# Blocks of zero matmuls on TensorE at four places of a one-core attention and feed-forward kernel

## Chip, cores and metric

The kernel runs on one core of a Trainium2 chip. The metric is the device time of one execution in microseconds (us), as the median of the runs. Engines are called PE (TensorE), DVE (VectorE), ACT (ScalarE), POOL (GpSimd) and SP (SyncE, here the engine that issues most DMAs); PEld is PE's weight load. PE's clock has two levels, 1.2 and 2.4 GHz; the profile shows the granted one as a fraction of full speed.

## What is computed

One layer on x of shape (2, 2048, 256): differential attention with 16 heads of width 16 (two score maps per head, values of width 32), then a gated feed-forward net with ternary weights, each followed by a residual sum and a layer norm. Cut to what matters:

```python
q1, q2, k1, k2 = (heads(x @ W) for W in (Wq1, Wq2, Wk1, Wk2)); v = heads(x @ Wv)
a1 = softmax(causal(q1 @ k1.T * scale)); a2 = softmax(causal(q2 @ k2.T * scale))
out = (a1 - lam * a2) @ v
out = (out - mean(out)) / sqrt(var(out) + eps) * (1 - LAM_INIT)
x = layernorm(x + merge(out) @ Wo)
h = silu((x @ w1.T) * s1) * ((x @ w2.T) * s2)
h = gelu((h @ h1.T) * hs1); h = gelu((h @ h2.T) * hs2)
x = layernorm(x + (h @ w3.T) * s3)
```

## The kernel before

The program is a row of phases, each a block with one instruction list per engine, written out by hand; between two blocks all engines meet at a barrier. The order on an engine is the order of the code, and engines wait for each other by semaphores only.

**Projection** (`project_phase`). The 4096 tokens are cut into 8 tiles of 512. For each tile PE makes eight m-tiles (q1, q2, k1, k2, two halves of 128 columns each), every one of six matmuls 128 x 512: two chunks of the width 256 by three passes, as each f32 operand is cut into a high and a low part (L479). It writes them to four PSUM banks in turn, so the fifth m-tile must wait until ACT has copied the first one out (L349). Between them come the four value tiles of L490. ACT makes the high parts of x (L333), wqk (L338) and wv (L340), DVE the low parts (L374, L378, L415); ahead of ACT's cast of wv DVE centres wv (L410, L412). ACT's queue has the cast of wv ahead of the first copy. At the end DVE takes the largest projection, POOL reduces it over the partitions (L324), and DVE sets a flag, `exact`, and the shift.

**The test of the exact path** (`maximum_phase`). Each engine loads the flag; when it is set, an extra phase finds the true row maxima. With these inputs it is not run, and only the load and the branch remain.

**Attention** (`attention_phase`). For each of 16 heads, PE makes scores into three PSUM slots (`scores`, L934), ACT takes the exponential of each (L908), POOL masks the corners on the diagonal (L880), and PE weighs the values (`weigh`, L957), DVE copies the sums, PE turns them (`turn`, L965), DVE finishes them. For the first head, the scores wait until DVE has added the shift to q (L1037). In the last head parts of the next stage for the first 512 tokens are done early: transposes (L977, L999) and the output projection (L987). The last thing on PE is the turn of the last query tile.

**Finish** (`finish_phase`). Each engine loads a second flag, `wide`. Then for 8 tiles of 512 tokens: the up-projections (L1525, 64 matmuls 128 x 512), two hidden layers (L1541, 256 matmuls), the down-projection (L1558), with the output projection and norm of the next tile in between. Small buffers of the norms come from `norm_buffers`.

Of the kernel before, what the change touches and what calls it, by code (L numbers as in the profile page):

```python
# [66 lines left out]
def layer_kernel(nc, x, xt, wqk, wv, wo, lq1, lk1, lq2, lk2, ffn, scales, s3, out):  # L67
# [7 lines left out]
    with ExitStack() as ctx:  # L75
        def sb(name, shape, dt=F32):
            return ctx.enter_context(nc.sbuf_tensor(name, shape, dt))

        keep = dict(
            scales=sb("scales", [PARTS, 4, HC]), counts=sb("counts", [PARTS, 2 * CHUNKS]), wide_col=sb("wide_col", [PARTS, 2]),
            s3=sb("s3", [PARTS, EMBED]),
            ident=sb("ident", [PARTS, PARTS]), neg_lam=sb("neg_lam", [PARTS, HEADS]),
            bound=sb("bound", [PARTS, 2]), exact=sb("exact", [PARTS, 1], I32), wide=sb("wide", [PARTS, 1], I32),
            low_rows=sb("low_rows", [PARTS, 2]), shift_row=sb("shift_row", [PARTS, 1]), safe_row=sb("safe_row", [PARTS, 1]),
            shift_add=sb("shift_add", [PARTS, 1]), query_rows=sb("query_rows", [PARTS, 1]),
        )
        for n, name in enumerate(("s1", "s2", "hs1", "hs2")):
            keep[name] = keep["scales"][:, n, :]  # L90
        finish = ctx.enter_context(Room(nc, "finish"))
        sems, finish_credits = finish_sems(finish)
        max_sems, max_credits = maximum_sems(finish)
        attn_sems, attn_credits = attention_sems(finish)
        with ExitStack() as weights:

            whole = weights.enter_context(nc.sbuf_tensor("ffn_r", [PARTS, CHUNKS, CHUNK], F32R))
            rounded = ffn_views(whole)
            early = early_buffers(nc)
            with Room(nc, "heads") as room:  # L100
                heads = first_head_buffers(room)
                project_phase(nc, keep, whole, heads, xt, wqk, wv, (lq1, lk1, lq2, lk2), ffn, (scales, s3),
                              qk_raw, values, shift, ones, finish_credits + max_credits + attn_credits)
                more_head_buffers(room, heads)
                maximum_phase(nc, keep, max_sems, heads, qk_raw, shift, ones)
                attention_phase(nc, keep, attn_sems, heads, early, qk_raw, shift, ones, values, ffn, whole, x, wo, diffs)
            finish_phase(nc, keep, sems, "split", True, rounded, early, attn_sems["stored"], x, wo, diffs, out)
        whole_w = sb("ffn_f", [PARTS, CHUNKS, CHUNK])
        load_weights_phase(nc, keep, ffn, whole_w)
        finish_phase(nc, keep, sems, "full", False, ffn_views(whole_w), None, attn_sems["stored"], x, wo, diffs, out)  # L110
# [30 lines left out]
        return self.ctx.enter_context(self.nc.Block())  # L141


def give_credits(eng, credits):

    for sem, n in credits:
        eng.sem_inc(sem, n)  # L147


def project_phase(nc, keep, rounded, heads, xt_in, wqk_in, wv_in, lam_in, ffn, ffn_s, qk_raw, values, shift, ones, later_credits):  # L150
# [13 lines left out]
    with Room(nc, "proj") as room:  # L164
# [25 lines left out]
        scales_loaded = room.sem("scales_loaded")  # L190
        x_loaded = [room.sem(f"x_loaded{u}") for u in range(2)]
        w_loaded = [room.sem(f"w_loaded{n}") for n in range(STAGES)]
        ident_done = room.sem("ident_done")
        preset_set = room.sem("preset_set")
        ones_stored = room.sem("ones_stored")
# [175 lines left out]
        def _(dve):  # L371
# [22 lines left out]
            def mark_rows():  # L394
# [6 lines left out]
                dve.wait_ge(row_vec, 2)  # L401
                nc.vector.scalar_tensor_tensor(keep["low_rows"][:, :], row_sums[:, :, 0], -1.0, row_sums[:, :, 1], ALU.mult, ALU.subtract).then_inc(row_vec, 1)

            low_x(0)
            for n in range(len(KINDS)):
                low_w(n)
# [55 lines left out]

        @block.tensor
        def _(pe):
            for t in range(TILES):

                pe.wait_ge(xt_ready, t + 1)
                for m in range(M_TILES):
# [14 lines left out]
                    if s is not None:  # L483
                        if t == 0:
                            pe.wait_ge(wv_ready, 1)
                        else:
                            pe.wait_ge(v_copied, SUBS * (t - 1) + s + 1)
                        for c in range(EC):
                            for i, (a, b) in enumerate(PASSES):
                                last = nc.tensor.matmul(v_ps[s][:, :, :], xt[t % 2][b][:, c, s * PARTS:(s + 1) * PARTS], wv[a][:, c * HEADS:(c + 1) * HEADS, :],  # L490
                                                        start=(c == 0 and i == 0), stop=(c == EC - 1 and i == len(PASSES) - 1))
                        last.then_inc(v_projected, 1)


def cut_piece(nc, dve, raw, stack, high, low_rows, made_high, i, made):
# [196 lines left out]

PROBS = 4
EARLY_PASSES = [(0, 0), (1, 0), (0, 1)]
EARLY_COLUMNS = 8448


def early_buffers(nc):
# [14 lines left out]

def norm_buffers(room, which):

    return dict(
        stats=room.sb(f"{which}_stats", [PARTS, SUBS, 6]), mean_var=room.sb(f"{which}_mean_var", [PARTS, SUBS, 2]),
        var=room.sb(f"{which}_var", [PARTS, SUBS]), root=room.sb(f"{which}_root", [PARTS, SUBS]),
        quotient=room.sb(f"{which}_quotient", [PARTS, SUBS]), rstd=room.sb(f"{which}_rstd", [PARTS, SUBS]),
    )  # L720


def attention_sems(room):
# [13 lines left out]
def attention_phase(nc, keep, sems, heads, early, qk_raw, shift, ones, values, ffn, rounded, x, wo, diffs):  # L737
# [44 lines left out]
    with Room(nc, "attn") as room:  # L782
# [128 lines left out]
        def _(pe):  # L911
# [105 lines left out]
            def head(h, u, r, first, last):  # L1017
# [5 lines left out]
                if last:  # L1023
                    for k in range(NS - LAG, NS):
                        use(h, u, first, k)
                    turn(h, QUERY_TILES - 1)

            all_heads(head)

        @block.vector  # L1030
# [817 lines left out]
```

## Time and profile before

| | us |
|---|---|
| median of 3 runs | 1936.9 |
| lowest, highest | 1936.12, 1937.7 |
| the profiled execution, its time | 1934.14 |
| the profiled execution, its span | 1932.4 |
| PE busy | 1858.1 |
| ACT busy | 1408.5 |
| DVE busy | 1027.1 |
| mean granted clock of PE | 0.985 |

The profile page, the chain of waits and the timeline come from that one execution. In a timeline row the first number is the start, the second the duration, both in us from the start of the span; then come the engine, the line, the operation, what it writes and reads, its shape and its count, and in brackets how long the engine was idle before it and what ended that. Rows of several instructions (x8) are merged: the duration is that of the whole. A name with q (SPq) is the engine's queue, here issuing DMAs. A row of windows gives a stretch, its length, the busy time of PE, PEld, DVE, ACT and POOL with the number of instructions, the granted clock of PE, the share of the DMA engines and GB/s. A clock of 0.50 is 1.2 GHz and 1.00 is 2.4 GHz; a number in between says at which point of the stretch it changed.

### The profile page before, as it was taken

What the parts mean: (1) busy time and instruction counts of PE and PEld (TensorE: products, weight loads), DVE (VectorE), ACT (ScalarE), POOL (GpSimd) and SP (SyncE); (2) the same over time, 40 slices, a digit from 0 to 9 for tenths busy, and PEclk for the clock granted to TensorE, in tenths of its full rate; (3) what the DMA queues carried; (4) which work ended last, traced back from release to release, by engine and by line L of the source; (5) the groups of instructions that cost most, each with busy time, mean ns of one, the idle gap of its engine ahead of it and who ended that gap; (6) DMA issues with size and microseconds to landing.
All of it is one profiled execution on the core that took longest, in us unless ns stands there. A gap on an engine that the chain in (4) does not pass through costs nothing. (4 is left out here: it accounts for less than half of the span.)

```text
span 1932.4 us, 30772 instructions
## 1 busy us (share of the span) xinstructions
PE 1858.1 (96%) x12160; PEld 1063.5 (55%) x12160; DVE 1027.1 (53%) x1985; ACT 1408.5 (73%) x1701; POOL 247.8 (13%) x311
## 2 busy tenths in 40 slices
PE   7997999999999999999999967999999999999996
PEld 6773333333333333333333323888888888888885
DVE  5555655555655665565555543535445454536342
ACT  4546999999999999999999965535445454535452
POOL 3001111211121111111122130000000000000000
PEclk9998999999999999999999988999999999999998
DMA  8877156534663357435653420010010001010000
GB/s 275 251 251 153 24 103 115 93 70 85 115 118 62 73 111 121 81 70 97 115 99 69 81 54 12 33 33 14 31 33 12 33 12 33 12 33 22 1 11 13
DMA packets 130143, 146.08 MB, mean 76 GB/s; under 512 B 74228, under 2 KB 100468, under 8 KB 122356
## 3 DMA queue, kind: packets, MB, share of 16 engines
q1 hardware_dynamic: 129272, 142.46, 34.1%
q8 instruction: 99, 1.62, 0.4%
q10 hardware_dynamic: 720, 1.57, 0.2%
q14 instruction: 52, 0.43, 0.1%
HBM read 101.79 MB, written 39.06 MB: 73 GB/s over the span
## 5 line engine op out<-in xcount | busy, mean ns | idle before, releaser
L908 ACT ACTIVATE attn_probs<-attn_s_ps 128x1024 f32<-128x1024 f32 x1088 | 1002.8, 1128 | 36.3 <-PE attn_s_ps L934 35.9
L957 PE MATMUL attn_sums_ps<-attn_probs,heads_v 128*32 128x512 f32 (+3 forms) x5120 | 589.8, 542 | 14.2 <-POOL attn_probs L880 14.2
L934 PE MATMUL attn_s_ps<-heads_q,heads_k 50*128 50x512 f32 (+3 forms) x2560 | 451.2, 427 | 12.5 <-DVE heads_q L1037 12.1
L934 PEld LDWEIGHTS attn_s_ps<-heads_q,heads_k 50*128 50x128 f32 x2560 | 213.1, 185 | 448.4 <-ACT attn_probs L908 401.7
L1627 ACT ACTIVATE split_whole<-split_hid_ps,scales 128x512 f32<-128x512 f32 x128 | 88.3, 690 | 274.2 <-PE split_hid_ps L1541 274.1
L880 POOL TENSOR_SCALAR_AFFINE_SELECT attn_probs<-attn_probs 128x512 f32<-128x512 f32 x256 | 182.9, 726 | 816.5 <-ACT attn_probs L908 816.5
L1541 PE MATMUL split_hid_ps<-split_hid_b,ffn_r 128*128 128x512 f32 x1024 | 240.8, 392 | 0.0
L1541 PE MATMUL split_hid_ps<-split_hid_a,ffn_r 128*128 128x512 f32 x1024 | 238.1, 391 | 0.0
L1541 PEld LDWEIGHTS split_hid_ps<-split_hid_a,ffn_r 128*128 128x128 f32 x1024 | 190.2, 188 | 41.1 <-DVE split_hid_a L1766 0.3
L957 PEld LDWEIGHTS attn_sums_ps<-attn_probs,heads_v 128*32 128x32 f32 x5120 | 107.9, 108 | 190.0 <-issue 157.4
L1541 PEld LDWEIGHTS split_hid_ps<-split_hid_b,ffn_r 128*128 128x128 f32 x1024 | 189.8, 188 | 38.2
L1772 DVE TENSOR_TENSOR split_hid_a<-split_whole,split_hid_a 128x512 fp32r<-128x512 f32 x64 | 44.3, 692 | 179.3 <-ACT split_hid_a L1630 179.2
L1079 DVE COPY attn_sums_sb<-attn_sums_ps 128x512 f32<-128x512 f32 x64 | 44.1, 690 | 172.1 <-PE attn_sums_ps L957 171.8
L1525 PE MATMUL split_hid_ps<-early_xt,ffn_r 128*128 128x512 f32 x512 | 121.3, 397 | 6.7 <-DVEq L147 6.7
L1084 DVE COPY attn_raw<-attn_sums_ps 128x512 f32<-128x512 f32 x64 | 44.2, 691 | 147.8 <-PE attn_sums_ps L965 147.8
L1525 PEld LDWEIGHTS split_hid_ps<-early_xt,ffn_r 128*128 128x128 f32 x512 | 94.0, 191 | 31.5 <-DVEq L147 6.9
L1612 ACT ACTIVATE split_gate<-split_hid_ps,scales 128x512 f32<-128x512 f32 x64 | 44.1, 688 | 88.8 <-PE split_hid_ps L1525 88.8
L1451 POOL TENSOR_TENSOR split_square<-early_heads 128x512 f32<-128x512 f32 x28 | 31.1, 1130 | 547.3 <-DVE split_head_var L1654 318.8
L499 DVE SCALAR_TENSOR_TENSOR heads_q<-heads_spare,query_rows,heads_q_raw 128x512 fp32r<-128x512 f32 x120 | 97.5, 813 | 4.3
L499 DVE SCALAR_TENSOR_TENSOR heads_k<-heads_spare,low_rows,heads_k_raw 128x512 fp32r<-128x512 f32 x128 | 97.1, 759 | 4.5
L1772 DVE TENSOR_TENSOR split_hid_b<-split_whole,split_hid_b 128x512 fp32r<-128x512 f32 x64 | 44.1, 689 | 94.9 <-ACT split_hid_b L1630 94.8
L497 DVE CAST heads_spare<-heads_k_raw 128x512 fp32r<-128x512 f32 x128 | 58.8, 459 | 41.5 <-DMA heads_k_raw<-ones 36.1
(166 smaller groups left out, 1673.6 us busy)
## 6 DMA issues: line engine op xcount, KB each, us to landing
heads_q_raw<-qk_raw SPq DMA_DIRECT2D x60, 384.0 KB
heads_k_raw<-qk_raw SPq DMA_DIRECT2D x60, 384.0 KB
qk_raw<-proj_copies SPq DMA_DIRECT2D x64, 256.0 KB, 2.7
values<-proj_v SPq DMA_DIRECT2D x8, 1024.0 KB, 6.5
diffs<-attn_diff SPq DMA_DIRECT2D x32, 256.0 KB, 4.1
heads_k_raw<-ones SPq DMA_DIRECT2D x60, 128.0 KB
heads_v<-values SPq DMA_DIRECT2D x15, 512.0 KB, 19.5
heads_spare<-in_ffn SPq DMA_DIRECT2D x30, 256.0 KB, 9.7
```

Source lines behind the costliest of these rows:

```text
L497: nc.vector.tensor_copy(high, raw).then_inc(made_high, 1)
L499: nc.vector.scalar_tensor_tensor(stack, high.bitcast(F32), low_rows, raw, ALU.mult, ALU.add).then_inc(made, 1)
L880: pool.affine_select(out=corner, in_=corner, compare_op=ALU.is_ge, fill=0.0, base=0, pattern=[[0, 2 * BATCH], [1, PARTS]], channel_multipl ...
L908: nc.scalar.activation(weights, side_by_side, ACT.Exp, scale=SCALE).then_inc(exp_done, 1)
L934: last = nc.tensor.matmul(s_ps[(NU * h + n) % SLOTS][:, s, col:col + width], k_sb[u][rows, b * SEQ + j * PARTS:b * SEQ + (j + 1) * PARTS], ...
L957: last = nc.tensor.matmul(sums[c * D:(c + 1) * D, off:TILE], v_sb[u][:, b * KEY_BLOCKS + j, :], probs[k % PROBS][:, b, s, place:place + wi ...
L1079: nc.vector.tensor_copy(sums_sb[:, :], sums_ps[t % 2][:, :]).then_inc(sums_copied, 1)
L1084: nc.vector.tensor_copy(raw[:, :, :, :].rearrange("p k s d -> p (k s d)"), sums_ps[t % 2][:, :]).then_inc(sums_bank_free, 1)
L1525: last = nc.tensor.matmul(bank[:, :], weights[w][:, c, m * PARTS:(m + 1) * PARTS], xt[k][:, c, :], start=(c == 0 and k == 0), stop=(c == E ...
L1541: last = nc.tensor.matmul(hid_ps[m % 4][:, :], weights[w][:, c, m * PARTS:(m + 1) * PARTS], hid[k][:, c, :], start=(c == 0 and k == 0), st ...
L1627: nc.scalar.activation(gelu, hid_ps[m % 4][:, :], ACT.Gelu, scale=keep[s][:, m:m + 1]).then_inc(gelu_done, 1)
L1772: nc.vector.tensor_tensor(hid[1][:, m, :], whole[m % 2][:, :], hid[0][:, m, :].bitcast(F32), ALU.subtract).then_inc(hid_low, 1)
```

## The change

A tile `zeros`, 128 x 128 in bf16, is set to zero by DVE as its first instruction. A new function runs a number of matmuls with it as both operands into a PSUM bank that nothing uses at that time:

- 60 at the start of PE's list in the projection, after a wait for the memset, into the fourth bank;
- 32 at the end of the projection, after a wait that the first bank has been copied, into that bank;
- 12 at the start of the attention, into the second bank of sums;
- 26 after the last turn of the last head, into the first slot of scores.

The new tile needs room, so `norm_buffers` makes slices of one tile instead of six tiles, and the finish phase's placeholder for the early buffers has 8432 columns instead of 8448.

```diff
+            zeros=sb("zeros", [PARTS, PARTS], BF16), ident=sb("ident", [PARTS, PARTS]), neg_lam=sb("neg_lam", [PARTS, HEADS]),
...
+def run_idle(nc, keep, bank, times):
+
+    for _ in range(times):
+        nc.tensor.matmul(bank[:, 0:PARTS], keep["zeros"][:, :], keep["zeros"][:, :], start=True, stop=True)
...
+            nc.vector.memset(keep["zeros"][:, :], 0.0).then_inc(zeros_set, 1)
             low_x(0)
...
         def _(pe):
+            pe.wait_ge(zeros_set, 1)
+            run_idle(nc, keep, qk_ps[BANKS - 1], 60)
             for t in range(TILES):
...
                         last.then_inc(v_projected, 1)
+            pe.wait_ge(qk_copied, M_TILES * TILES - BANKS + 1)
+            run_idle(nc, keep, qk_ps[0], 32)
...
-EARLY_COLUMNS = 8448
+EARLY_COLUMNS = 8432
...
-    return dict(
-        stats=room.sb(f"{which}_stats", [PARTS, SUBS, 6]), mean_var=room.sb(f"{which}_mean_var", [PARTS, SUBS, 2]),
-        var=room.sb(f"{which}_var", [PARTS, SUBS]), root=room.sb(f"{which}_root", [PARTS, SUBS]),
-        quotient=room.sb(f"{which}_quotient", [PARTS, SUBS]), rstd=room.sb(f"{which}_rstd", [PARTS, SUBS]),
-    )
+    whole = room.sb(f"{which}_norm", [PARTS, 12 * SUBS])
+    ends = {"stats": (0, 6), "mean_var": (6, 8), "var": (8, 9), "root": (9, 10), "quotient": (10, 11), "rstd": (11, 12)}
+    bufs = {name: whole[:, a * SUBS:b * SUBS] for name, (a, b) in ends.items()}
+    for name in ("stats", "mean_var"):
+        bufs[name] = bufs[name].rearrange("p (s n) -> p s n", s=SUBS)
+    return bufs
...
                     turn(h, QUERY_TILES - 1)
-
+                    run_idle(nc, keep, s_ps[0][:, 0, :], 26)
+
+            run_idle(nc, keep, sums_ps[1], 12)
             all_heads(head)
```

PE at the beginning of the projection, before:

```order
L463 UNCONDITIONAL_BRANCH [waits barrier_Pool_Activation_PE_DVE_SP_release]
L479 MATMUL proj_qk_ps<-proj_xt_high,proj_wqk_high 128x512 [waits proj_wqk_ready,proj_xt_ready]
L479 MATMUL proj_qk_ps<-proj_xt_high,proj_wqk_low 128x512
L479 MATMUL proj_qk_ps<-proj_xt_low,proj_wqk_high 128x512
L479 MATMUL proj_qk_ps<-proj_xt_high,proj_wqk_high 128x512
```

and now, where the lines of the changed kernel are counted:

```order
L471 UNCONDITIONAL_BRANCH [waits barrier_Pool_Activation_PE_DVE_SP_release]
L147 MATMUL proj_qk_ps<-zeros 128x128 [waits proj_zeros_set]
L147 MATMUL proj_qk_ps<-zeros 128x128 x59
L489 MATMUL proj_qk_ps<-proj_xt_high,proj_wqk_high 128x512 [waits proj_wqk_ready,proj_xt_ready]
L489 MATMUL proj_qk_ps<-proj_xt_high,proj_wqk_low 128x512
```

Sixty matmuls now stand ahead of the first projection matmul, and their one wait is for the memset.

PE at the end of the projection and at the load of the flag `exact`, before:

```order
L479 MATMUL proj_qk_ps<-proj_xt_high,proj_wqk_high 128x512
L479 MATMUL proj_qk_ps<-proj_xt_high,proj_wqk_low 128x512
L479 MATMUL proj_qk_ps<-proj_xt_low,proj_wqk_high 128x512
L123 UNCONDITIONAL_BRANCH
L628 UNCONDITIONAL_BRANCH [waits barrier_Pool_Activation_PE_DVE_SP_release]
L630 TENSOR_LOAD exact
```

and now:

```order
L489 MATMUL proj_qk_ps<-proj_xt_low,proj_wqk_high 128x512
L147 MATMUL proj_qk_ps<-zeros 128x128 [waits proj_qk_copied]
L147 MATMUL proj_qk_ps<-zeros 128x128 x31
L123 UNCONDITIONAL_BRANCH
L640 UNCONDITIONAL_BRANCH [waits barrier_Pool_Activation_PE_DVE_SP_release]
L642 TENSOR_LOAD exact
```

The 32 stand ahead of the barrier and the flag's load; the 12 stand behind it, ahead of the attention's first scores.

PE at the end of the attention and at the start of the finish phase, before:

```order
L999 MATMUL attn_sums_ps<-ident,early_mid 128x128 x4
L965 MATMUL attn_sums_ps<-ident,attn_sums_sb 128x128 x4
L123 UNCONDITIONAL_BRANCH
L1460 UNCONDITIONAL_BRANCH
L1386 TENSOR_LOAD wide
L1387 COMPARE_AND_BRANCH
L1525 MATMUL split_hid_ps<-early_xt,ffn_r 128x512 x64
```

and now:

```order
L1012 MATMUL attn_sums_ps<-ident,early_mid 128x128 x4
L978 MATMUL attn_sums_ps<-ident,attn_sums_sb 128x128 x4
L147 MATMUL attn_s_ps<-zeros 128x128 x26
L123 UNCONDITIONAL_BRANCH
L1475 UNCONDITIONAL_BRANCH
L1401 TENSOR_LOAD wide
L1402 COMPARE_AND_BRANCH
L1540 MATMUL split_hid_ps<-early_xt,ffn_r 128x512 x64
```

The 26 stand between the last transposes and the barrier; the up-projection's 64 matmuls are as before.

## Rows read from the trace of the kernel before

**Rows 1.** The page: PE's busy time, and the granted clock in 40 slices.

```profile
PE 1858.1 (96%) x12160; PEld 1063.5 (55%) x12160; DVE 1027.1 (53%) x1985; ACT 1408.5 (73%) x1701; POOL 247.8 (13%) x311
...
PEclk9998999999999999999999988999999999999998
```

**Rows 2.** The chain of waits in order of time: start, us, what.

```profile
1206.49 16.96 PE split_hid_ps L1525 x64
...
1298.42 14.74 PE split_hid_ps L1525 x64
```

**Rows 3.** Timeline of PE at the beginning.

```profile
8.21 0.77 PE L479 MATMUL proj_qk_ps<-proj_xt_high,proj_wqk_high 128*128 128x512 f32 x1 [8.21 <-DVE proj_wqk_low L378]
...
11.76 0.63 PE L479 MATMUL proj_qk_ps<-proj_xt_low,proj_wqk_high 128*128 128x512 f32 x1
12.19 0.63 PE L479 MATMUL proj_qk_ps<-proj_xt_high,proj_wqk_high 128*128 128x512 f32 x1
...
15.70 0.40 PE L479 MATMUL proj_qk_ps<-proj_xt_low,proj_wqk_high 128*128 128x512 f32 x1
17.45 0.47 PE L479 MATMUL proj_qk_ps<-proj_xt_high,proj_wqk_high 128*128 128x512 f32 x1 [1.35 <-ACT proj_copies L349]
```

**Rows 4.** Timeline of DVE and ACT at the beginning.

```profile
8.37 0.69 DVE L378 TENSOR_TENSOR proj_wqk_low<-proj_wqk_low_raw,proj_wqk_high 128x512 fp32r<-128x512 f32 x1 [0.31 <-ACT proj_wqk_high L338]
...
13.26 1.22 DVE L410 TENSOR_REDUCE proj_wv_mean<-proj_wv_low_raw 128x32 f32<-128x1024 f32 x1 [0.81 <-DMA proj_wv_low_raw<-in_wv]
...
15.78 1.05 ACT L340 CAST proj_wv_high<-proj_wv_low_raw 128x1024 fp32r<-128x1024 f32 x1 [4.05 <-DVE proj_wv_low_raw L412]
16.73 1.07 ACT L349 COPY proj_copies<-proj_qk_ps 128x512 f32<-128x512 f32 x2
```

**Rows 5.** Windows: the projection after its first tiles.

```profile
20.00:149.00 129.00, 127.60 (x541) 100.90 (x540) 72.04 (x119) 63.84 (x105) 4.00 (x8) 1.00 0.81 254
```

**Rows 6.** Timeline from the last projection matmul to the first scores.

```profile
149.32 0.39 PE L479 MATMUL proj_qk_ps<-proj_xt_low,proj_wqk_high 128*128 128x512 f32 x1
...
152.02 0.57 SPq L274 DMA_DIRECT2D qk_raw<-proj_copies  x1
...
159.51 0.10 POOL L870 MEMSET attn_half<- 128x1 f32 x1 [7.63 <-POOLq L123]
...
161.14 1.65 PE L934 MATMUL attn_s_ps<-heads_q,heads_k 50*128 50x512 f32 x8 [11.43 <-DVE heads_q L1037]
```

**Rows 7.** Windows: the five stretches in which the granted clock changes.

```profile
152.50:152.75 0.25, 0.00 (x0) 0.00 (x0) 0.18 (x2) 0.00 (x0) 0.00 (x0) 0.76 0.40 74
169.60:169.80 0.20, 0.20 (x8) 0.00 (x0) 0.09 (x1) 0.20 (x1) 0.00 (x0) 0.76 1.56 246
...
1190.20:1190.40 0.20, 0.00 (x0) 0.00 (x0) 0.00 (x0) 0.00 (x0) 0.20 (x1) 0.70 0.00 0
1203.75:1204.00 0.25, 0.00 (x0) 0.00 (x0) 0.00 (x0) 0.00 (x0) 0.00 (x0) 0.87 0.00 0
1210.75:1211.00 0.25, 0.25 (x2) 0.21 (x2) 0.00 (x0) 0.22 (x1) 0.00 (x0) 0.98 1.10 393
```

**Rows 8.** Timeline of PE and SP at the attention's end.

```profile
1187.39 1.06 PE L957 MATMUL attn_sums_ps<-attn_probs,heads_v 128*32 128x512 f32 x8
...
1193.93 1.11 PE L999 MATMUL attn_sums_ps<-ident,early_mid 128*128 128x128 f32 x4 [5.48 <-DVE early_mid L1207]
...
1199.19 0.66 PE L965 MATMUL attn_sums_ps<-ident,attn_sums_sb 128*128 128x128 f32 x4 [0.24 <-DVE attn_sums_sb L1079]
...
1203.30 1.29 SPq L862 DMA_DIRECT2D diffs<-attn_diff  x2
```

**Rows 9.** Timeline: POOL's first work of the projection.

```profile
0.80 1.84 POOL L301 MEMSET proj_v<- 128x1024 f32 x2 [0.29 <-POOLq L1838]
```

**Rows 10.** Timeline of PE and ACT early in the attention.

```profile
166.61 1.93 PE L957 MATMUL attn_sums_ps<-attn_probs,heads_v 128*32 128x512 f32 x8
...
169.37 1.02 ACT L908 ACTIVATE attn_probs<-attn_s_ps 128x1024 f32<-128x1024 f32 x1 [0.81 <-PE attn_s_ps L934]
```

More of the change, by code:

```diff
@@ L83, in layer_kernel @@
             s3=sb("s3", [PARTS, EMBED]),
-            ident=sb("ident", [PARTS, PARTS]), neg_lam=sb("neg_lam", [PARTS, HEADS]),
+            zeros=sb("zeros", [PARTS, PARTS], BF16), ident=sb("ident", [PARTS, PARTS]), neg_lam=sb("neg_lam", [PARTS, HEADS]),
             bound=sb("bound", [PARTS, 2]), exact=sb("exact", [PARTS, 1], I32), wide=sb("wide", [PARTS, 1], I32),
@@ L192, in project_phase @@
         w_loaded = [room.sem(f"w_loaded{n}") for n in range(STAGES)]
+        zeros_set = room.sem("zeros_set")
         ident_done = room.sem("ident_done")
```

## The prediction

> **What bounds the kernel now.** I read the page first. TensorE (PE) is busy for 96% of the span, and its granted clock is at or near full in nearly every slice [rows 1]. So there is little low clock to win back: the question is where PE stands, what the clock does there, and whether PE is what the stage waits for. The chain of waits says that from 1206 us to the end PE is the path: the first group of 64 up-projection matmuls takes 16.96 us, the same group of the next tile 14.74 us [rows 2]. These 2.2 us are the dearest price of a low clock that I find on the path.
>
> Then the timeline, at the places that the change touches, and the clock in short windows.
>
> *The beginning.* The first projection matmul starts at 8.21 us. Neighbours start 0.43 us apart (11.76, 12.19), which is 512 columns at 1.2 GHz; at full clock the spacing is 14.74/64 = 0.23 us. (The granted-clock column reads 1.00 here; no change of clock is recorded before 152 us, so I go by the spacing.) The 24th matmul ends at 16.10 and the 25th starts at 17.45, released by ScalarE's (ACT) first copy [rows 2, 3]. That copy begins at 16.73, right behind ACT's cast of wv, which waits for a chain on VectorE (DVE) that begins when wv has landed, at 13.26 [rows 4]. Nothing of that chain depends on PE. From there PE is busy 127.6 of 129 us [rows 5]: a loss on PE after 17.45 is a loss for the stage.
>
> *Around the test of the exact path.* The last projection matmul ends at 149.71, the sync engine (SP) issues its last store until 152.59, and the first work of the attention stands at 159.51. PE begins at 161.14, when DVE has added the shift [rows 6].
>
> *The clock.* It falls at 152.6, 1190.3 and 1203.9, that is 2.9, 1.8 and 4.1 us after the last matmul before it (149.71, 1188.45, 1199.85). It rises at 169.7 and 1210.8, so 8.6 and 4.3 us after PE had begun again [rows 2, 6 to 8]. (One more fall lies in a stall of the last head that the change doesn't touch.)
>
> **The change, part by part.**
>
> *Price of one zero matmul.* No 128-column bf16 matmul is in the trace. A quarter of the 512-column spacing is 0.107 us at the low level and 0.058 at the high one [rows 2, 3]. The other bound is the f32 transpose of 128 columns, weight load included: 1.11/4 = 0.28 and 0.66/4 = 0.165 us [rows 8]. I take the lower one, since the 512-column rows too have a weight load each and hide it, and since f32 operands are wider than bf16. The Trainium skill (TensorE: Matmul & The Clock Gate, "Wait — 56ns, not 53.3ns?") gives 106.7 and 55.6 ns from start to start for such matmuls; with these the sum stays as it is.
>
> *60 at the beginning.* DVE's memset is first in its queue, in time in which it had nothing to do. The block runs from about 1 us, since the first work of the program stands at 0.80 [rows 9], for at most 60 x 0.107 = 6.4 us, to 7.4, before 8.21. Say it raises the clock: the 24 matmuls then take 24 x 0.23 = 5.5 us instead of 7.9, if no weights are late (the twelve from the 13th on need the second kind's, which DVE has cut at 9.06) [rows 4]. Their end moves to about 13.8, and the 25th still waits for ACT until 17.45. Gain: 0. What grows is the gap in front of the 25th matmul, from 1.35 to about 3.6 us; a rival below prices it.
>
> *32 behind the projection.* The semaphore they wait for, the copy of the bank's last tile, is four copies old by then. 32 x 0.058 = 1.9 us brings PE to 151.6, before SP's 152.59 [rows 6]: hidden, with 1 us to spare. From 151.6 to 159.5 PE stands for 8 us, far more than the 4.1 us after which the clock had fallen at the latest: it falls anyway. Gain 0.
>
> *12 ahead of the attention.* From about 159.5 they take 12 x 0.107 = 1.3 us, to 160.8, before the 161.14 at which DVE releases the first scores. PE is thus active 1.6 us earlier, and the clock may rise earlier than 169.7. What is that worth? ACT sets the pace here, and it waited for PE once, 0.81 us at 169.37, behind eight value matmuls that took 1.93 us at the low clock where others take 1.06 [rows 8, 10]. The gain lies between 0 and 0.8; I take the middle, 0.4, as the block may come too early or too late for the rise.
>
> *26 behind the last turn.* 26 x 0.058 = 1.5 us, from 1199.85 to 1201.35, while SP issues its stores until 1204.59 [rows 8]: hidden. The gap to 1206.49 shrinks from 6.6 to 5.1 us. The three falls came after 1.8 to 4.1 us, all shorter than 5.1, so the clock is most likely low again when the up-projection begins. Gain 0, at the other bound 2.2 us [rows 2].
>
> *The rest.* The norm buffers become slices of one tile and the early buffers' columns shrink by 16; the instructions on them are the same in number and shape. DVE, ACT, POOL and SP get no new wait. Cost 0.
>
> Sum: 0 + 0 - 0.4 + 0 = -0.4 us. The profiled execution took 1934.14 us (its span is 1932.4), 2.8 below the median of the runs, 1936.9. As the terms are differences, I put them on the median: 1936.9 - 0.4 = **1936.5 us**. Against the profiled execution's own time the same sum gives 1933.7.
>
> **The rivals.**
>
> *The lengthened gap costs the clock (slower).* PE now runs ahead at the beginning and then stands 3.6 us. Two of the three falls came after less than that (1.8 and 2.9 us); the gap of 1.35 us before did not bring one: the matmuls right after 17.45 are spaced at full clock and the page shows no fall. If the clock falls, the 25th matmul starts low, and a low stretch like the one at 1206.49 costs 2.2 us, which this PE-bound stage hides nowhere [rows 2, 5]. Time: 1936.5 + 2.2 = 1938.7. The Trainium skill (same page, "Why this matters for your kernels") has the rule that idle gaps between bursts of matmuls put the clock back, so keeping PE fed earlier only moves the gap; its result is this rival's. It speaks against the first part of the change.
>
> *The clock lives through the shortened gap at the end (faster).* One fall came 4.1 us after the last matmul, so 5.1 us is near enough to escape some of the time. Then 2.2 us more go: 1936.5 - 2.2 = 1934.3; with the full 0.8 at the attention's start 1933.9.
>
> *The zeros do nothing.* Should a block of zeros not raise the clock, or end just where it can't matter, every part is hidden work: 1936.9.
>
> *The zero matmuls are dear (slower by over 0.2%).* At the transposes' price the 60 would last 16.7 us and end at 17.7; the 24 matmuls behind them end 5.5 us later at the best, at 23.2 instead of 17.3, the moment from which they delay: +5.9. The 32 would end 5.3 us after 149.71, 2.4 us behind SP; the 12 at 162.9, 1.7 us late. Together up to 10 us: 1946.9. It decides from 0.18 us apiece on (10.7 us for 60, so that 24 x 0.23 still fit before 17.3). Against it: the projection's weight loads cost nothing visible.
>
> **How the numbers follow.** The forecast has 0.45, the lost clock at the beginning 0.27, the kept clock at the end 0.15, no effect 0.09, dear zeros 0.04. Differences below 0.2%, 3.9 us, can hardly be told from none. Faster by more than that is under 1933.0: it needs the kept clock, the full gain at the start of attention and luck, 0.04. Slower by more is over 1940.8: the dear zeros, or a lost clock that stays low for longer than 4.3 us, 0.05. The rest, 0.91, is within 0.2%. The range reaches from the kept clock to the lost clock, each with the 0.8 us by which the runs stray from their median: 1933.5 (from 1934.3) to 1939.5 (from 1938.7).
>
> **What would show it.** In the profile of the changed kernel: the 24 first projection matmuls 0.23 us apart and the 25th still released by ACT near 17.4; the spacing right behind it tells the first rival (0.23 or 0.43). The zero matmuls 0.107 and 0.058 us apart. The clock low from about 154.5, and ACT's wait of 0.81 near 169 gone or shorter. The clock at the first up-projection matmul low, and its 64 matmuls again near 17 us; 14.8 would be the second rival. I am wrong if the total moves by over 3.9 us, which would mean that the start of a stage hangs on PE by a way that I have not seen, or that the price of a zero matmul is over 0.18 us.

## The result, and the profile after

| | before | after |
|---|---|---|
| median, us | 1937.3 (6 runs, 1936.12 to 1939.83) | 1949.59 (6 runs, 1948.22 to 1950.48) |
| profiled execution: time, span | 1934.14, 1932.4 | 1950.14, 1948.4 |
| mean granted clock of PE | 0.985 | 0.984 |

The changed kernel is slower by 12.3 us: the ratio is 1.0063, with a 95% interval of 1.0053 to 1.0074. The forecast was 1936.5 and its range ended at 1939.5. So the time lies outside the range and beyond every rival, the dearest (1946.9 us, from dear zero matmuls, with a chance of 0.04) included, and that one did not happen either.

The page after looks like the one before [rows 1]. PE is busy 20.7 us more, and the granted clock is the same row of digits:

```profile
PE 1878.8 (96%) x12290; PEld 1071.2 (55%) x12290; DVE 1028.2 (53%) x1986; ACT 1408.6 (72%) x1701; POOL 246.6 (13%) x311
...
PEclk9998999999999999999999988999999999999998
```

**Where the time is.** The chain of waits of the two kernels through the first tile of the finish phase (start us, us, what); first before, of which the hidden layers' rows are shown:

```profile
1223.45 21.82 PE split_hid_ps L1541 x96
...
1271.09 14.54 PE split_hid_ps L1541 x64
```

then after:

```profile
1211.46 17.14 PE split_hid_ps L1540 x64
1228.60 22.41 PE split_hid_ps L1556 x96
...
1277.14 14.94 PE split_hid_ps L1556 x64
...
1304.84 14.73 PE split_hid_ps L1540 x64
```

The up-projection takes what it took [rows 2]: 17.14 against 16.96 us at the low clock, 14.73 against 14.74 at the high one. The hidden layers (L1541 before, L1556 after) do not: the same 96 matmuls take 22.41 us instead of 21.82, the same 64 take 14.94 instead of 14.54. From start to start that is 233 ns instead of 227. No wait stands in these pieces and the clock is at full; each single matmul is slower. There are 2048 of them, and 2048 x 5.55 ns (the difference of the mean distances from start to start in these layers, 234.82 and 229.27) is 11.4 us. The groups by operands say the same; before:

```profile
L1541 PE MATMUL split_hid_ps<-split_hid_b,ffn_r 128*128 128x512 f32 x1024 | 240.8, 392 | 0.0
L1541 PE MATMUL split_hid_ps<-split_hid_a,ffn_r 128*128 128x512 f32 x1024 | 238.1, 391 | 0.0
...
L1558 PE MATMUL split_y_ps<-ffn_r,split_hid_a 128*128 128x256 f32 x512 | 64.7, 284 | 2.8 <-DVE split_y L1796 2.8
```

and after:

```profile
L1556 PE MATMUL split_hid_ps<-split_hid_b,ffn_r 128*128 128x512 f32 x1024 | 246.5, 396 | 0.0
L1556 PE MATMUL split_hid_ps<-split_hid_a,ffn_r 128*128 128x512 f32 x1024 | 243.7, 396 | 0.0
...
L1573 PE MATMUL split_y_ps<-ffn_r,split_hid_a 128*128 128x256 f32 x512 | 63.8, 281 | 2.8 <-DVE split_y L1811 2.8
```

Each hidden layer takes 5.6 to 5.7 us more of busy time; the down-projection, which has the hid tile as its weights and moves a piece of `ffn_r`, takes 0.9 less. From the first up-projection matmul to the end of the span it is 736.9 us after and 725.9 before: 11.0 us of the 16.0 by which the spans differ. The other 5.0 us are gone before 1211.46.

**The beginning.** PE's timeline after, to be held against [rows 3]:

```profile
1.05 4.99 PE L147 MATMUL proj_qk_ps<-zeros 128*128 128x128 bf16 x60 [1.05 <-DVE zeros L411]
8.67 0.47 PE L489 MATMUL proj_qk_ps<-proj_xt_high,proj_wqk_high 128*128 128x512 f32 x1 [2.63 <-DVE proj_wqk_low L385]
...
13.89 0.40 PE L489 MATMUL proj_qk_ps<-proj_xt_high,proj_wqk_low 128*128 128x512 f32 x1
14.13 0.40 PE L489 MATMUL proj_qk_ps<-proj_xt_low,proj_wqk_high 128*128 128x512 f32 x1
17.84 0.76 PE L489 MATMUL proj_qk_ps<-proj_xt_high,proj_wqk_high 128*128 128x512 f32 x1 [3.32 <-ACT proj_copies L356]
18.40 0.63 PE L489 MATMUL proj_qk_ps<-proj_xt_high,proj_wqk_low 128*128 128x512 f32 x1
```

The clock rises at 4.16 us, within the 60, and the 24 matmuls are 0.23 us apart instead of 0.43. The 25th still waits for ACT's first copy, so what was gained is a gap of 3.32 us instead of 1.35, and behind it the spacing is 0.43 again: the clock is low from 17.81 to 21.23 us (in the window 17.75 to 18.00 below, the last figure but two is its mean, 0.63). The nine matmuls from the 25th take 3.71 us from the first start to the start of the tenth, where before they took 2.16. (The 25th comes at 17.84 instead of 17.45 since ACT's copy does; ACT issued its first DMAs in 2.59 instead of 2.13 us in this execution.)

```profile
17.75:18.00 0.25, 0.16 (x1) 0.19 (x2) 0.25 (x1) 0.25 (x1) 0.09 (x1) 0.63 0.76 311
```

**The attention's start**, against [rows 6]:

```profile
162.05 0.69 PE L147 MATMUL attn_sums_ps<-zeros 128*128 128x128 bf16 x5 [7.83 <-PEq L123]
165.02 0.91 PE L147 MATMUL attn_sums_ps<-zeros 128*128 128x128 bf16 x7 [2.28 <-issue]
165.85 1.44 PE L947 MATMUL attn_s_ps<-heads_q,heads_k 50*128 50x512 f32 x6
```

The first scores start at 165.85 instead of 161.14 us, +4.71. Of these, 2.5 were there already (POOL's first work stands at 162.01 instead of 159.51). The other 2.2 are a hole in the middle of the 12 zero matmuls. The profile puts it down to "issue": PE waits there for nothing that the profile shows. From there to the attention's end the two kernels keep step.

**The attention's end**, against [rows 8] and [rows 2]: the 26 take 1.61 us and hide, but the gap ahead of the up-projection is still 5.18 us long, and in it the clock falls at 1209.06, 2.4 us before the up-projection begins:

```profile
1204.66 1.61 PE L147 MATMUL attn_s_ps<-zeros 128*128 128x128 bf16 x26
1211.46 2.05 PE L1540 MATMUL split_hid_ps<-early_xt,ffn_r 128*128 128x512 f32 x4 [5.18 <-DVEq L153]
```

### The profile page after: what moved, and what is told of

Read it like the earlier page. It is cut to its first block and busy times, and to the rows that moved or that the text cites. A ratio compares the mean times of both kernels' runs of the same rounds, so it can differ in the third digit from the quotient of the medians.

```text
span 1948.4 us, 31033 instructions
## 1 busy us (share of the span) xinstructions
PE 1878.8 (96%) x12290; PEld 1071.2 (55%) x12290; DVE 1028.2 (53%) x1986; ACT 1408.6 (72%) x1701; POOL 246.6 (13%) x311
## 5 line engine op out<-in xcount | busy, mean ns | idle before, releaser
L970 PE MATMUL attn_sums_ps<-attn_probs,heads_v 128*32 128x512 f32 (+3 forms) x5120 | 590.1, 542 | 13.8 <-POOL attn_probs L893 13.8
L1556 PE MATMUL split_hid_ps<-split_hid_b,ffn_r 128*128 128x512 f32 x1024 | 246.5, 396 | 0.0
L1556 PE MATMUL split_hid_ps<-split_hid_a,ffn_r 128*128 128x512 f32 x1024 | 243.7, 396 | 0.0
L1556 PEld LDWEIGHTS split_hid_ps<-split_hid_a,ffn_r 128*128 128x128 f32 x1024 | 190.3, 188 | 46.2 <-DVE split_whole L1777 0.8
L1556 PEld LDWEIGHTS split_hid_ps<-split_hid_b,ffn_r 128*128 128x128 f32 x1024 | 189.3, 188 | 43.9
```

Of the source, the lines that this page charges most:

```text
L970: last = nc.tensor.matmul(sums[c * D:(c + 1) * D, off:TILE], v_sb[u][:, b * KEY_BLOCKS + j, :], probs[k % PROBS][:, b, s, place:place + wi ...
L1556: last = nc.tensor.matmul(hid_ps[m % 4][:, :], weights[w][:, c, m * PARTS:(m + 1) * PARTS], hid[k][:, c, :], start=(c == 0 and k == 0), st ...
```

## The experiments

The theory: the FFN is slower because its tiles moved in SBUF. The new tile `zeros` is 256 bytes per partition and stands ahead of nearly everything, so all later tiles move up by 256; the shorter placeholder takes 64 bytes back for the tiles of the finish phase that stand behind it, hid among them. By the program's table of addresses the weights `ffn_r` start at 288 modulo 1024 before and 544 after, `hid_a` and `hid_b` at 544 before and 736 after. The distance from the start of the weights to the start of the moving tile is 256 bytes before and 192 after. The rest (5 us) I put down to the clock at the beginning and the hole at the attention's start. The rival: the zero matmuls themselves, or what they do to the clock, slow the FFN.

The experiments are numbered as their labels (e1 to e12). Below, "spacing" is the time of an uninterrupted group of 96 or 64 of the hidden layers' matmuls in the chain of waits, divided by their number (before 227 ns, in the changed kernel 233), and "the FFN" the time from the first up-projection matmul to the span's end. Where a kernel uses "before's addresses", its block of zeros is a tile of its own in each phase, placed behind all other tiles (in the attention POOL sets it to zero).

### 1. The new layout without the zero matmuls

```diff
-            run_idle(nc, keep, qk_ps[BANKS - 1], 60)
+            run_idle(nc, keep, qk_ps[BANKS - 1], 0)
```

(and likewise the 32, 26 and 12).

> The change with its four blocks of zero matmuls emptied: what is left is the zeros tile in the buffers that are kept, its memset, the one tile of statistics per norm, and EARLY_COLUMNS at 8432. Theory (addresses): the slower matmuls of the FFN (L1556 of the changed kernel, 233 to 234 ns from start to start where the kernel before had 227) come from where its tiles lie in SBUF; then this kernel has that spacing too, its FFN lasts 737 us instead of 726, and it stands 10 to 12 us above the kernel before (about 1948 us). Rival (the zero matmuls or TensorE's clock slow the FFN): 227 ns, FFN 726 us, and the time of before, 1937 us. The projection and the exact path's branch stand as before in either case.

1947.25 us against 1937.18 for the kernel before beside it, ratio 1.0055 (1.0038 to 1.0072). Its FFN takes 737.1 us, and its groups are those of the changed kernel to the last digit:

```profile
L1556 PE MATMUL split_hid_ps<-split_hid_b,ffn_r 128*128 128x512 f32 x1024 | 246.5, 396 | 0.0
L1556 PE MATMUL split_hid_ps<-split_hid_a,ffn_r 128*128 128x512 f32 x1024 | 243.7, 396 | 0.0
```

Ten of the twelve us come without a single zero matmul.

### 2. The zero matmuls without the new layout

```diff
+        zeros = room.sb("zeros", [PARTS, PARTS], BF16)
...
+            run_idle(nc, zeros, qk_ps[BANKS - 1], 60)
```

(the other three blocks as in the change; the tile is the last of its phase, the norm buffers and the placeholder are before's).

> The kernel before with all four blocks (60, 32, 12, 26), while every tile that it had keeps its address: the block of zeros is a tile of its own in each of the two phases, behind all others. Theory (addresses for the FFN, clock and branch for the rest): FFN spacing 227 ns and length 726 us; the clock falls in the gap before the 25th projection matmul, which costs 2.3 to 2.7 us; the hole between the 5th or 6th and the next of the 12 costs 0 to 2.2 us more; together 3 to 5 us above before, about 1941 us. Rival (the zero matmuls slow the FFN): 12 us above before, about 1949 us, with 233 ns.

1939.86 us, ratio 1.0016 (1.0006 to 1.0026), +2.7 us, where 3 to 5 had been expected. Spacing 227 ns, FFN 727.5 us. The two parts add up: 10.1 + 2.7 = 12.8 us, against 12.3 for the whole change.

### 3. The 60 alone

> The 60 at the beginning alone, all of before's tiles at before's addresses. Theory: the clock falls in the gap before the 25th projection matmul (3.3 us in the changed kernel) and the projection ends 2.3 to 2.7 us later; nothing else differs, so about 1939.5 us. Rival (the early clock gives back what the later fall costs): within 0.5 us of before. The FFN at 227 ns in either case.

1938.42 us, ratio 1.0006 (0.9995 to 1.0017). In the profiled execution the gap was there, and the clock did not fall in it:

```profile
13.93 0.39 PE L490 MATMUL proj_qk_ps<-proj_xt_low,proj_wqk_high 128*128 128x512 f32 x1
17.52 0.47 PE L490 MATMUL proj_qk_ps<-proj_xt_high,proj_wqk_high 128*128 128x512 f32 x1 [3.20 <-ACT proj_copies L357]
```

The nine matmuls from the 25th took 2.17 us, as without the 60. Of the five profiles with the 60 and this gap unfilled, four (the changed kernel, runs 2, 4 and 10) show the fall and 3.45 to 3.71 us for the nine, this one does not. So the expected cost of 2.3 to 2.7 us was too high twice: when the clock falls it is 1.3 to 1.6 us, and it doesn't always fall. The total, 1.2 us above before, can't tell this from zero.

### 4. The change with the hid tiles 64 bytes higher

```diff
-EARLY_COLUMNS = 8432
+EARLY_COLUMNS = 8448
```

> The change as it is, with EARLY_COLUMNS at 8448 again instead of 8432, which moves the FFN's hid tiles 64 bytes up and nothing below them: hid then starts 256 bytes after ffn_r modulo 1024, as in the kernel before, not 192. Theory A (the distance between the two operands decides): spacing back at 227 ns, FFN 726 us, about 1938.5 us to 1941 us in all. Theory B (where one of them lies decides, or something else than hid's address): 233 ns and 1949 us, as the changed kernel.

1941.62 us, ratio 1.0023 (1.0013 to 1.0032): 8 us below the changed kernel's 1949.59, by one number. `hid_a` and `hid_b` are now at 800 modulo 1024, 256 behind the weights again, and both groups are back at before's:

```profile
L1556 PE MATMUL split_hid_ps<-split_hid_b,ffn_r 128*128 128x512 f32 x1024 | 240.8, 392 | 0.0
L1556 PE MATMUL split_hid_ps<-split_hid_a,ffn_r 128*128 128x512 f32 x1024 | 237.9, 391 | 0.0
```

The spacing is that of theory A; the time, 4.4 us above before, is slightly more than its 1938.5 to 1941. The constant moves every tile behind the placeholder, so that it is the hid tiles that matter is only likely here; runs 5, 6 and 9 show it, as two layers differ there within one kernel. And both tiles were also at 32 modulo 128 in the good kernels and at 96 in the bad one, so their own place was not excluded.

### 5, 6 and 9. Which distances are good

Three kernels without zero matmuls, with padding; runs 6 and 9 also have the change's norm buffers and its shorter placeholder. Two layers can be at two distances in one kernel, since the first hidden layer reads `hid_a` and the second `hid_b`. The edit of run 5:

```diff
+            pad=sb("pad", [PARTS, 16]), scales=sb("scales", [PARTS, 4, HC]), ...
...
         hid_a = [room.sb(f"hid_a{k}", [PARTS, HC, TILE], part_type) for k in range(CUTS)]
+        room.sb("pad_b", [PARTS, 16])
         hid_b = [room.sb(f"hid_b{k}", [PARTS, HC, TILE], part_type) for k in range(CUTS)]
```

> The kernel before with 64 unused bytes ahead of all tiles and 64 more between hid_a and hid_b: ffn_r starts at 352 modulo 1024 (before: 288), hid_a at 608, hid_b at 672 (both 544 before). Theory A (the distance between the weights and the moving tile decides): the layer that reads hid_a, distance 256 as before, keeps 227 ns from start to start; the layer that reads hid_b, distance 320, shows something else, 233 if every distance other than 256 is bad. Theory B (where hid itself lies decides; 544 and 800 were good, 736 bad, which are 32, 32 and 96 modulo 128): hid_a, now at 96 modulo 128, takes 233 ns and hid_b, at 32, takes 227. The time moves by 5 to 6 us per layer at 233: about 1942 us in both theories.

> The kernel before with the compacted norm buffers, the shorter placeholder, and padding ahead of hid_a and hid_b that puts them 224 and 384 bytes behind ffn_r modulo 1024 (256 both before, 192 in the changed kernel). Theory A1 (multiples of 128 or 256 are good): 224 shows 230 ns or more, 384 shows 227. Theory A2 (256 and more is good, less is bad): 224 shows 230 ns or more and 384 shows 227 as well, while the distance 320 of the run beside it shows 227 too; A1 wants 233 there. Theory B of that run: hid_a at 512 and hid_b at 672, 0 and 32 modulo 128, so hid_b at 227. Time between 1937 and 1948 us.

> The kernel before with the compacted norm buffers, the shorter placeholder and padding that puts hid_a 448 and hid_b 512 bytes behind ffn_r modulo 1024. Seen so far at the hidden layers: 256 gives 227 ns from start to start (14.5 us for 64 matmuls), while 192, 224, 320 and 384 give 232 to 233 ns (14.9 us). Theory 1 (multiples of 256 are good): the layer on hid_a at 233 ns (96 matmuls in 22.4 us), the layer on hid_b at 227 ns (64 in 14.5 us). Theory 2 (256 alone is good, or a band around it): both at 232 ns or more.

Times 1942.87, 1943.36 and 1944.90 us, one run each. The chain of waits of the first:

```profile
1227.56 21.86 PE split_hid_ps L1542 x96
...
1275.34 14.94 PE split_hid_ps L1542 x64
```

of the second:

```profile
1224.36 22.40 PE split_hid_ps L1544 x96
...
1272.82 14.87 PE split_hid_ps L1544 x64
```

and of the third:

```profile
1229.55 22.40 PE split_hid_ps L1544 x96
1277.89 14.54 PE split_hid_ps L1544 x64
```

The x96 belong to the layer that reads `hid_a`, the x64 to the one that reads `hid_b`. All distances are of the start of the moving tile from the start of the weights, modulo 1024:

| distance | kernels | 96 matmuls, us | 64 matmuls, us |
|---|---|---|---|
| 192 | change, run 1 | 22.39 to 22.41 | 14.94 |
| 224 | run 6 | 22.40 | |
| 256 | before, runs 4, 5 | 21.82 to 21.86 | 14.54 |
| 320 | run 5 | | 14.94 |
| 384 | run 6 | | 14.87 |
| 448 | run 9 | 22.40 | |
| 512 | run 9 | | 14.54 |

In run 5 `hid_a` lies at 96 modulo 128 and is fast, `hid_b` at 32 and is slow: theory B as it was put, with places modulo 128, falls. The distance explains all rows. Multiples of 64 or 128 are not enough (320 and 384 are slow), the two multiples of 256 are good. Both theories of run 6 had expected 227 ns at 384 and missed; the first one of run 9 came true. This is shown for these matmuls (128 x 512 in f32r, weights from one tile, moving data from the other) and for distances from 192 to 512.

Two things stay open. The first is a rule on hid's own place with a longer period. Modulo 1024 the fast hid tiles lay at 544, 608 and 800 (32, 96 and 32 modulo 256), the slow ones at 512, 672 and 736 (0, 160 and 224), and no place was seen both fast and slow. So a rule like "32 to 96 modulo 256 is fast" fits as well, and no run has one hid place at a good and at a bad distance. For the distance speaks that it needs one rule only, and that in run 5 `ffn_r` and `hid_a` moved by 64 bytes together and kept their 227 ns. The second is the period of the distance: one matmul's weights are a piece of `ffn_r`, and these pieces stand 512 bytes apart, so the rows can't tell modulo 1024 from modulo 512 or 256.

The up-projections read all their tiles from the early `xt`, at distance 0 in all kernels, and take 14.7 us for 64 in all of them. Why the distance matters is not shown by any run. One thing goes the other way: the down-projection, with `hid_a` as its weights and 256 columns moving, has 64.7 us of busy time where `hid_a` is at 256 and 63.3 to 63.8 at 192, 224 and 448.

### 7. The 12 alone

> The 12 zero matmuls at the attention's start alone, all of before's tiles at before's addresses. Theory (the instructions behind the fifth of the 12 come late): PE starts the 12 near 159.6 us, stands 2.2 to 2.6 us behind the fifth or sixth, and the first scores start near 163.4 us instead of 161.1; the clock rises up to 2 us earlier in relation to them; 1938 to 1939.5 us in all. Rival (the hole came from the 32 in front of the barrier or from the kept tile's memset): the 12 run in one piece for 1.3 us, the first scores stay at 161.1 us, time as before or 0.4 us less.

The rival is right. 1936.52 us (one run, against 1936.69 for before beside it); the 12 run in one piece and the first scores stay where they were:

```profile
159.64 1.46 PE L147 MATMUL attn_sums_ps<-attn_zeros 128*128 128x128 bf16 x12 [10.07 <-POOL attn_zeros L881]
161.03 1.65 PE L946 MATMUL attn_s_ps<-heads_q,heads_k 50*128 50x512 f32 x8
```

They bring nothing that can be seen either: the clock rises at 172.13 us, 11.1 us after the first scores, where before it rose 8.6 us after them. (That is no loss by the 12: over all profiles it rises 8.3 to 14.0 us after the first scores without them and 9.0 to 13.8 with them.) ACT waits for PE at the same place, 0.79 us instead of 0.81 [rows 10]. So the hole needs something that stands in front.

### 10. 28 instead of 32

```diff
-            run_idle(nc, zeros, qk_ps[0], 32)
+            run_idle(nc, zeros, qk_ps[0], 28)
```

> The four blocks at before's addresses with 28 zero matmuls instead of 32 behind the projection, so everything behind them stands four matmuls (with their weight loads) earlier in PE's code. With 60, 32 and 12 PE stood 2.2 to 2.6 us behind the fifth of the 12; with the 12 alone it did not stand. Theory (the hole lies at a fixed place of PE's code, where the next piece has to be fetched): the hole now lies behind the ninth of the 12. Rival (it is a matter of time since the barrier, or of the blocks in front of it, whatever their number): it stays behind the fifth. Time about 1939 to 1941 us in both.

1939.30 us (one run). The timelines of run 2, with 32, and of this one:

```profile
162.43 0.71 PE L147 MATMUL attn_sums_ps<-attn_zeros 128*128 128x128 bf16 x5 [8.21 <-POOL attn_zeros L886]
165.00 0.93 PE L147 MATMUL attn_sums_ps<-attn_zeros 128*128 128x128 bf16 x7 [1.86 <-issue]
```

```profile
161.56 1.14 PE L147 MATMUL attn_sums_ps<-attn_zeros 128*128 128x128 bf16 x9 [8.15 <-POOL attn_zeros L886]
164.05 0.50 PE L147 MATMUL attn_sums_ps<-attn_zeros 128*128 128x128 bf16 x3 [1.35 <-issue]
```

Four matmuls less in front, and the hole moves from behind the fifth (so in the changed kernel and in runs 2 and 4) to behind the ninth. It is tied to a place in PE's code. In a window of the changed kernel over the hole, the DMA view shows one packet on an instruction queue:

```profile
q8 instruction: 1, 0.02, 1.2%
```

It begins at 162.32 and lasts 1.23 us, right after PE entered the phase at 162.01; in the kernel before one of the same size begins 0.40 us after PE's entry too, but there PE stands until 161.14 for DVE anyway. My guess is that PE reaches the end of the code that it has before the next piece is there, since the zero matmuls need no data and run it through at once. That the hole follows the code's place is shown. The packet as its cause is not: the hole ends 1.5 us after it, and in run 7 such a packet begins 0.35 us after the phase's start too, with no hole.

### 11. The gap at the beginning filled

```diff
+                    if n == BANKS:
+                        run_idle(nc, zeros, v_ps[SUBS - 1].rearrange("p h d -> p (h d)"), 44)
```

> The 60 at the beginning and 44 more between the 24th and the 25th projection matmul, into a bank of the values that is not in use yet; before's addresses. The 44 take 2.4 us of the 3.6 us gap. Theory (the gap made the clock fall at 17 us, and that is all that the 60 cost): no fall before 150 us, the matmuls behind the 25th 0.23 us apart, the projection ends near 149.8 us as before, and the time is that of before, 1937 us. Rival (the 60 themselves cost or bring something): off by more than 1 us in the projection's end.

1936.11 us, ratio 1.0000 (0.9991 to 1.0010):

```profile
14.22 2.63 PE L147 MATMUL proj_v_ps<-proj_zeros 128*128 128x128 bf16 x44
17.55 0.50 PE L492 MATMUL proj_qk_ps<-proj_xt_high,proj_wqk_high 128*128 128x512 f32 x1 [0.70 <-ACT proj_copies L357]
17.88 0.39 PE L492 MATMUL proj_qk_ps<-proj_xt_high,proj_wqk_low 128*128 128x512 f32 x1
```

No fall before 153.41 us, nine matmuls in 2.21 us, and the projection ends at 149.85. With the clock kept from 6.6 us on, the beginning is worth what it was: the 25th matmul waits for ACT in any case. In this place the 60 can only cost.

### 8 and 12. Zeros where a low clock costs something

The trace of before has three gaps of PE in the last head with a fall in them and PE's own work behind: 14.2 us before 1140.82 (PE waits for a mask of POOL, which is busy with a root for 10.57 us), 5.5 us before 1193.93, 6.65 us before 1206.49. Both kernels keep before's addresses and have none of the change's blocks but the last, made longer.

```diff
+                if c == 0:
+                    pe.wait_ge(exp_done, NU * (LAST + 1) - 2)
+                    run_idle(nc, zeros, s_ps[(NU * (LAST + 1) - 3) % SLOTS][:, 0, :], 80)
                 pe.wait_ge(early_mid_ready, SUBS)
...
                     turn(h, QUERY_TILES - 1)
+                    run_idle(nc, zeros, s_ps[0][:, 0, :], 78)
```

and in the second one also, ahead of `weigh`:

```diff
+                if h == LAST and k == VAR_AT + 2:
+                    n = next(n for n, (step, _) in enumerate(UNITS) if step == k + LAG + 1)
+                    pe.wait_ge(exp_done, NU * h + n - SLOTS + 1)
+                    run_idle(nc, zeros, s_ps[(NU * h + n) % SLOTS][:, 0, :], 220)
```

> A version that puts zero matmuls where a fall of the clock costs something and PE has nothing else: none at the beginning, at the projection's end and at the attention's start; 80 ahead of the first transposes of early_mid in the last head (gap of 5.5 us before, so some 1 us of it is left) and 78 instead of 26 behind the last turn (4.3 us of the 6.65 us gap; more would hold up the barrier behind SP's last issue). All tiles of before at before's addresses. Theory: the clock does not fall at 1190 us, so PE's 4.5 us of work from 1193.9 take 1.6 us less, and with luck not at 1204 either, which gives 2.2 us at the first up-projection: 1935.5 us with the first alone, 1933.5 with both. Rival (the clock falls in the 1 us and the 2.3 us that are left, or at 1204 all the same): 1937 us. Rival 2 (PE comes late to the transposes or the barrier): over 1938 us.

> The version with 80 and 78 zero matmuls in the last head's gaps and, in addition, 220 of them (12.2 us) in the gap of 13.9 us ahead of the value matmuls that wait for POOL's mask at 1140 us in the last head. Theory: the clock no longer falls at 1128.8 us, so the scores, value matmuls and transposes between 1140 and 1146 us run at full clock, for which ACT waits twice (14.7 and 1.07 us): 1 to 2 us less than without the 220, that is 1931.5 to 1932.5 us, 4 to 5 us under the kernel before. Rival (ACT's or DVE's own work sets the pace there): as without the 220, 1933.5 us.

The first: 1933.56 us, ratio 0.9986 (0.9976 to 0.9996), as expected with both gaps held. The second, also as expected: 1932.14 us against 1937.0 beside it, ratio 0.9973 (0.9965 to 0.9982). It beats both kernels: 4.9 us under before and some 17 under the change. In its trace the clock falls twice only, behind the projection and behind the last matmul; the page's row:

```profile
PEclk9998999999999999999999999999999999999998
```

and its timeline from 1188 us on, against [rows 2], [rows 8] and this row of before:

```profile
1194.98 3.38 PE L957 MATMUL attn_sums_ps<-attn_probs,heads_v 128*32 128x256 f32 x24
```

```profile
1188.49 4.64 PE L147 MATMUL attn_s_ps<-attn_zeros 128*128 128x128 bf16 x80
1193.85 0.66 PE L1011 MATMUL attn_sums_ps<-ident,early_mid 128*128 128x128 f32 x4 [0.72 <-DVE early_mid L1225]
1194.44 2.35 PE L966 MATMUL attn_sums_ps<-attn_probs,heads_v 128*32 128x256 f32 x24
...
1198.10 4.52 PE L147 MATMUL attn_s_ps<-attn_zeros 128*128 128x128 bf16 x78
1204.91 15.19 PE L1543 MATMUL split_hid_ps<-early_xt,ffn_r 128*128 128x512 f32 x64 [2.29 <-DVEq L153]
```

The transposes take 0.66 instead of 1.11 us, the 24 value matmuls 2.35 instead of 3.38, and the first 64 up-projection matmuls 15.19 instead of 16.96 (15.20 in the first of the two). The two windows over the stall at 1140, before and then in this kernel (stretch, length, busy time of PE, PEld, DVE, ACT, POOL, granted clock, DMA share, GB/s), show the third piece, a clock of 1.00 instead of 0.63:

```profile
1125.00:1148.00 23.00, 8.82 (x52) 2.96 (x52) 6.94 (x15) 7.23 (x9) 12.06 (x3) 0.63 0.01 2
```

```profile
1125.00:1148.00 23.00, 21.37 (x299) 15.70 (x296) 7.79 (x14) 9.31 (x11) 11.19 (x2) 1.00 0.08 31
```

ACT's waits for scores there, 14.70, 1.07 and 0.31 us in run 8, are a single one of 13.69 in run 12. In the totals the third piece can't be told apart: 4.9 us under before against 3.1, with intervals that overlap.

## Why the prediction was wrong, and where it was right

**The step that failed** is the shortest one, "The rest": "the instructions on them are the same in number and shape [...] Cost 0". Number and shape are the same, the addresses are not. Moving the tiles cost 10.1 us (run 1), five sixths of the whole, and one constant takes back 8 (run 4): each of the hidden layers' 2048 matmuls takes 5.5 ns more in the new places, with no wait and no low clock. The prediction knew of the new tile and of the smaller buffers, and priced only instructions, not where the tiles come to lie. No rival covered it; "dear zeros" came nearest in time, but the zero matmuls cost 107 and 56 ns apiece, about as taken (0.107 and 0.058 us).

**The first rival happened** in part: the lengthened gap lost the clock in four of five profiles. Its price was 1.3 to 1.6 us, not 2.2: the low stretch lasted 3.42 us, while PE worked 4.3 us at the low clock where the price was taken from. That a gap of this length does not always bring the fall is seen in run 3. The Trainium skill (TensorE: Matmul & The Clock Gate, "Why this matters for your kernels") says that idle gaps between bursts put the clock back; the traces agree in four cases of five with an idle gap of 2.6 to 3.3 us (the fifth, run 3, had 3.2). In runs 8, 11 and 12 no fall came where 0.7 to 1.3 us of idle were left, nor where 2.3 to 2.8 us were left ahead of the up-projection.

**60 at the beginning, gain 0**: right. The 24 matmuls took 0.23 us each and ACT released the 25th. Run 11 shows that even without the fall nothing is gained (ratio 1.0000).

**32 behind the projection, gain 0**: hidden as said (they end near 154.0, SP's last issue at 154.64), and the clock fell all the same, at 157.76. What was missed is their length in PE's code: with four of them less the hole in the 12 moves by four matmuls (run 10), and without them and the 60 there is none (run 7).

**12 ahead of the attention, -0.4**: wrong. Alone they bring nothing in the profile of run 7, and the total can't tell 0.4 us; behind the other blocks they cost 2.2 us in the changed kernel's profile.

**26 behind the last turn, gain 0**: right, with the reason given. The gap left was 5.18 us and the 64 matmuls took 17.14. The second rival needed more zeros: with 78 the gap left is 2.8 us and the clock lives (run 8).

**The sum** of the changed kernel's profile against before's, 16.0 us: 11.0 in the FFN; 2.7 by the end of the projection, of which 1.55 are the nine slow matmuls, 0.4 ACT's slower start and some 0.8 a wait for DVE at 117 us that other kernels with the same projection have too (run 12, for one, and there the projection ends at 152.14); 2.2 for the hole; the rest is below what two single profiles can tell. The medians differ by less, 12.3, mainly because before's profiled execution was 3.2 us under its median. Before's own runs reach from 1933.2 to 1941.6 us, and they go with the clock: in one set the three with a mean granted clock of 0.982 took 1939.9 us on average, the four with 0.985 took 1935.4. So the 0.8 us of stray in the stated range, taken from three runs, was too small as well, though by far too little to explain the miss.

## What to carry to other kernels

A new tile is a change to every tile behind it. Where one engine is busy for most of the time with one kind of instruction, compare that instruction's start-to-start time before and after any change of the layout, and try a pad before you put the difference down to the edit itself. Filling PE's idle time pays only where the low clock stands on the path behind the gap, and the filling must reach nearly to the gap's end (2.8 us left was short enough here, 5.2 was not); where the work behind the gap waits for data anyway it brought nothing, and could cost.

## What the runs showed of the hardware that I had not expected

- The spacing of 128 x 512 f32r matmuls depends on where weights and moving data lie: 227 ns with 256 and 512 bytes (modulo 1024) between the starts of the two tiles, 232 to 233 ns with 192, 224, 320, 384 and 448. A rule on the moving tile's own place modulo 256 fits the same rows.
- The matmuls with the roles changed (256 columns moving) are slightly faster at the distances that are bad for the others: 281 against 284 ns mean duration.
- Twelve matmuls that need no data can be stopped for 1.4 to 2.4 us in their middle (four profiles), at a place that moves with the number of matmuls in front of them.
- Blocks of zero matmuls hold the clock over waits of 5 to 14 us; in the profiled execution of run 12 it was 0.993 on the mean instead of 0.985.
